# Differential attention in a four-layer sandwich: PSUM banks moved from the scores for the exponentials to the natural scores

## The reference

```
q1, k1, q2, k2, v = split(x @ Wqkv)      # 16 heads of 8; v: 16 heads of 16
A1 = softmax(mask(q1 k1^T / sqrt(8))) v  # causal, 1024 x 1024 per head and batch
A2 = softmax(mask(q2 k2^T / sqrt(8))) v
diff = A1 - lam * A2
out  = rmsnorm(diff per head) * (1 - lambda_init) @ Wproj
```

## Time and profile before

| | us |
|---|---|
| median of 3 runs | 1840.18 |
| lowest and highest | 1839.37, 1842.9 |
| the profiled execution, its own time | 1842.77 |
| its span, first to last instruction | 1841.0 |

### The profile page before, as it was taken

The page is one execution under the profiler, slowest core; times in us unless marked ns, Lnnn a source line. Parts: engine busy times, 40 slices in busy tenths (PEclk is TensorE's granted clock), DMA queues, the critical chain, the costliest instruction groups (busy, mean ns, idle before and its releaser), DMA issues. The chain is left out here.

```text
span 1841.0 us, 29946 instructions
## 1 busy us (share of the span) xinstructions
PE 1528.2 (83%) x8470; PEld 1026.0 (56%) x8532; DVE 1297.8 (70%) x3447; ACT 1086.2 (59%) x2348; POOL 1095.9 (60%) x1272
## 2 busy tenths in 40 slices
PE   4758989989989974377885789999999999989798
PEld 2413333333333323256563578888888888877566
DVE  5458777777777712483426599999999999984443
ACT  1104666666666661030222389999999999996241
POOL 5211456556456474301324399999999999984253
PEclk9858999999999996698998899999999999999899
DMA  3310100100101000383210000000000010000000
GB/s 114 120 51 24 32 19 24 29 18 25 28 18 25 12 1 1 126 274 103 92 46 1 1 1 1 1 1 1 1 1 1 1 46 1 1 1 1 1 23 23
DMA packets 39162, 59.48 MB, mean 32 GB/s; under 512 B 8700, under 2 KB 33160, under 8 KB 38152
## 3 DMA queue, kind: packets, MB, share of 16 engines
q1 hardware_dynamic: 39048, 58.12, 9.9%
HBM read 40.93 MB, written 16.78 MB: 31 GB/s over the span
## 5 line engine op out<-in xcount | busy, mean ns | idle before, releaser
L1896 POOL TENSOR_SCALAR c_R<-c_Z,c_negtau 128x256 f32<-128x256 f32 x519 | 589.0, 1167 | 53.3 <-DVE c_negtau L1965 30.8
L588 ACT ACTIVATE a_PT<-a_sc 128x512 f32<-128x512 f32 x576 | 316.3, 602 | 258.2 <-PE a_sc L653 174.9
L493 DVE TENSOR_REDUCE a_mpart<-a_nat 128x1 f32<-128x512 f32 (+3 forms) x640 | 378.0, 632 | 124.8 <-PE a_nat L620 78.4
L1851 ACT ACTIVATE c_R<-c_Z,c_negtau 128x256 f32<-128x256 f32 x1017 | 425.5, 515 | 5.2 <-DVE c_negtau L1965 3.4
L1932 DVE BATCH_NORM_STATS2 c_stat<-c_R 128x6 f32<-128x512 f32 x576 | 380.8, 678 | 2.7 <-ACT c_R L1851 2.7
L617 PE MATMUL a_nat<-KS,QS 96*128 96x512 bf16 (+3 forms) x768 | 253.5, 348 | 78.2 <-DVE a_mpart L493 44.9
L460 POOL TENSOR_SCALAR_AFFINE_SELECT a_PT<-a_PT 128x512 f32<-128x512 f32 x128 | 79.1, 636 | 265.1 <-ACT a_PT L588 265.1
L1768 PE MATMUL c_z<-mem,c_R 128*128 128x256 f32 x1024 | 231.5, 379 | 0.0
L1768 PEld LDWEIGHTS c_z<-mem,c_R 128*128 128x128 f32 x1024 | 193.1, 190 | 25.4
L653 PE MATMUL a_sc<-QS,KS 128*128 128x512 bf16 (+3 forms) x706 | 194.3, 324 | 3.9 <-ACT a_PT L588 2.9
L617 PEld LDWEIGHTS a_nat<-KS,QS 96*128 96x128 bf16 x768 | 74.5, 98 | 201.1 <-DVE a_mpart L493 161.0
(11 more groups left out here) (319 smaller groups left out, 2238.1 us busy)
## 6 DMA issues: line engine op xcount, KB each, us to landing
qk_parts<-a_parts SPq DMA_DIRECT2D x4, 1536.0 KB, 5.9
QS<-qk_parts SPq DMA_DIRECT2D x192, 32.0 KB
KS<-qk_parts SPq DMA_DIRECT2D x192, 32.0 KB
made<-m_made SPq DMA_DIRECT2D x24, 256.0 KB, 4.0
mem<-made SPq DMA_DIRECT2D x3, 2048.0 KB, 8.2
X<-in_L_attn_x_dram SPq DMA_DIRECT2D x1, 2048.0 KB, 8.5
ternary<-a_W_T SPq DMA_DIRECT2D x1, 2048.0 KB, 6.3
mem<-in_L_ffn_wq_dram SPq DMA_DIRECT2D x1, 2048.0 KB, 14.6
```

Source lines behind the costliest of these rows:

```text
L493: dve.tensor_reduce(mpart[:, b, j:j + cnt, i, k0 // 512], src, AX.X, ALU.max).then_inc(s_max, 1)
L588: act.activation(PT[:, n % 3, c, :], sc[:, u % 3, :], ACT.Exp, scale=SCALE0).then_inc(s_exp, 1)
L1851: act.activation(split(i, h) if r < NR else whole(i, h), Z[:, slot(i), h, :], ACT.Relu, bias=threshold(i, r, h)).then_inc(s_ra[r], 1)
L1896: pool.tensor_scalar(split(i, h) if r < NR else whole(i, h), Z[:, slot(i), h, :], threshold(i, r, h), 0.0, ALU.add, ALU.max).then_inc(s_rp ...
```

## The change

The tile `nat` gets three PSUM banks instead of two, and `sc` two instead of three; the sum stays eight banks. A unit now waits for the reduction three before, a score for the exponential two before. Since 40 is no multiple of 3, the bank of a unit is counted over the heads (`h.k` is the head's place in the loop).

```diff
-        nat, sc, OT, misc = ps("nat", [P, 2, 512]), ps("sc", [P, 3, 512]), ps("OT", [P, T]), ps("misc", [P, 512])
+        nat, sc, OT, misc = ps("nat", [P, 3, 512]), ps("sc", [P, 2, 512]), ps("OT", [P, T]), ps("misc", [P, 512])
...
-                src = nat[:, u % 2, 0:cnt * w].rearrange("p (a w) -> p a w", a=cnt)
+                src = nat[:, (NU * h.k + u) % 3, 0:cnt * w].rearrange("p (a w) -> p a w", a=cnt)
...
-                        act.activation(PT[:, n % 3, c, :], sc[:, u % 3, :], ACT.Exp, scale=SCALE0).then_inc(s_exp, 1)
+                        act.activation(PT[:, n % 3, c, :], sc[:, u % 2, :], ACT.Exp, scale=SCALE0).then_inc(s_exp, 1)
...
-                if not isinstance(h.n, int) or NU * h.n + u > 1:
-                    pe.wait_ge(s_max, h.count(NU, u - 1))
+                if not isinstance(h.n, int) or NU * h.n + u > 2:
+                    pe.wait_ge(s_max, h.count(NU, u - 2))
...
-                    out = nat[:, u % 2, s * w:(s + 1) * w]
+                    out = nat[:, (NU * h.k + u) % 3, s * w:(s + 1) * w]
...
-                if not isinstance(h.n, int) or 4 * NCH * h.n + u > 2:
-                    pe.wait_ge(s_exp, h.count(4 * NCH, u - 2))
+                if not isinstance(h.n, int) or 4 * NCH * h.n + u > 1:
+                    pe.wait_ge(s_exp, h.count(4 * NCH, u - 1))
...
-                    ins = pe.matmul(sc[:, u % 3, col:col + w], KS[:, h.buf, j, b * T + kt * P:b * T + (kt + 1) * P],
+                    ins = pe.matmul(sc[:, u % 2, col:col + w], KS[:, h.buf, j, b * T + kt * P:b * T + (kt + 1) * P],
```

## The result

| | before | after |
|---|---|---|
| median (lowest to highest), four runs each, us | 1841.54 (1839.37 to 1842.96) | 1791.21 (1788.79 to 1792.48) |
| profiled execution, own time / span | 1842.77 / 1841.0 | 1788.79 / 1787.0 |
| TensorE busy, VectorE busy | 1528.2, 1297.8 | 1519.5, 1288.3 |
| mean granted TensorE clock | 0.936 | 0.943 |

The ratio is 0.9716, 95% interval 0.9701 to 0.9731: **faster by 50.3 us**. The forecast was 38.3 faster, 1802, with a range from 1792. The sign and the mechanism held, the size did not: one stretch was priced at a seventh of its worth. The result lies just under the range, where rival 1 had put it (1791), and the first question is whether for its reason.

A forecast was written before the change was run, and what follows sets the result against it. No engine is full; TensorE idles 5.5 of 34.3 us a period, waiting mainly for VectorE to free natural banks. Savings 36.4 + 2.0 + 1.0 - 1.1 = 38.3 us gave a 1802 median, range 1792 to 1817.

The forecast's parts named there:

- rival 1: New waits for ScalarE and GpSimd hardly show, so 3.6 us a period is saved: 1791 us, chance 0.10.
- So the third bank of `sc` is not used up, and the second of `nat` is too few: Attention stage: TensorE's natural scores wait for VectorE 312 times; nearly all 61 score waits for ScalarE cost nothing.
- The replay of the period: One attention period of nine matmul groups, replayed with the new bank waits: 3.0 us saved of 34.26, chance 0.64.
- Group 9: Five units after VectorE's split, 4.31 us before: two come at once, four later waits stay, 0.25 saved.
- I take a new wait of 0.2 a period: Values of chunk 7 wait for GpSimd's mask: 0.2 us a period, between 0 and 0.6.
- The units before 165 us are mostly bound by VectorE or a load: 1.0, between 0 and 1.5.: Natural units ahead of the periods: the third bank saves only 1.0 us there, between 0 and 1.5.
- In head 0's period ... 2.0: First head's period, without VectorE's outputs between: group 7 saves only 0.24 us, the period 2.0.
- In the last head ... a loss of 1.1: Last head, no units to save on: groups grow by 0.54 us, mostly covered by GpSimd waits; 1.1 lost.
- Late work elsewhere: Rival: GpSimd's chain, or VectorE behind it, costs 1.0 us a period more: 1815 us, chance 0.18.
- the score ring deciding: Rival: TensorE's waits for exponentials in each group outweigh the gain, 4.9 us a period against 3.6: about 1857, chance 0.04.
- no change: Rival: TensorE's waits only turn into others, VectorE being the true bound: 1840 us, chance 0.03.
- The clock one: Rival: a tenth of the stretch at the lower, half-speed clock level costs 40 us: 1842, chance 0.01.

The follow-up runs named there:

- e3: The changed kernel with natural units waiting as with two banks throughout, so both rings use two: 1841.77 us, ratio 1.0001 to the kernel before.
- e1: The changed kernel with natural units waiting as with two banks in the ramp (ahead of the first exponential) only: 1798.11 us, ratio 0.9761 to the kernel before.
- e2: The changed kernel with the third natural bank used in the ramp only, two in the periods: 1833.61 us, ratio 0.9959 to the kernel before.
- e5: The changed kernel with GpSimd's ternary block in two parts, earlier, behind the masks of chunks 0 and 2: 1782.68 us, ratio 0.9700 to the kernel before.
- e4: The changed kernel with VectorE's outputs (reciprocal and product) moved behind the ninth unit of the next head: 1790.94 us, ratio 0.9721 to the kernel before.
- e6: The changed kernel with both the moves of e4 and e5, outputs later and ternary block earlier: 1781.95 us, ratio 0.9696 to the kernel before.
- e7: The kernel before, with only VectorE's reciprocal and product moved as in e4: 1829.01 us, ratio 0.9953 to the kernel before.

## Why the prediction was right, and where it was wrong

- *"So the third bank of `sc` is not used up, and the second of `nat` is too few"*: right. e3 puts the one at about nothing, and e1 and e2 share the 50 us of the other between the ramp and the periods.
- *The replay of the period*: right in eight of nine groups to 0.07 us, and in the starts of c0 and c1. Its sum was 31.5 with the wait for GpSimd, and the measured period is 31.44. That this fits so closely is partly luck: group 9 was 0.28 too short in it and the wait 0.2 too long, and the two cancel.
- *Group 9*: 4.06 forecast, 4.34 measured. VectorE's split took 1.37 us before (376.50 to 377.87). It took 1.57 after, and VectorE went into it without the pause of 0.91 that it had in the kernel before, so no cushion took the difference up. e5, where the split is 0.25 shorter and nothing else in the group differs, has 4.09; e4 and e6, where the outputs are elsewhere and the pause is back, have 4.06 and 3.96.
- *"I take a new wait of 0.2 a period" for GpSimd*: the place was right, the values of chunk 7 start 16.3 after group 7, where 16.25 was worked out, but the wait is hardly there: 0.05 in one period of three (group 2: 3.50 for 3.45). e4 shows that the slack is used up: ask for the values sooner and the wait grows by nearly as much as had been won.
- **The step that failed**: *"The units before 165 us are mostly bound by VectorE or a load: 1.0, between 0 and 1.5."* It is worth 7.1 by the trace, about 8 by e1 and 7.6 by e2. The bound was read from merged rows, which looked like work without a gap, and the bank's round trip that the replay used in the periods was never worked out at the lower clock level, where a matmul of 512 columns takes 0.43 instead of 0.22. There the two-bank ring allowed 0.70 a unit against VectorE's 0.56. Over the 40 units of head 0 this is 27.59 - 22.40 = 5.2, and 1.9 more on those of the next head.
- *"In head 0's period ... 2.0"*: 3.2 up to the first copy of the sums. 2.1 of it lie behind the first block of values, as forecast; 1.2 lie ahead of it (the next score starts at 157.98 and 148.36, 8.51 and 7.35 after the first exponential). Part of the 1.2 is the clock's: the upper level came about 3.5 us after the first exponential before and 2.3 after it now (0.74 granted from 152.50 to 153.50 before, 0.84 from 143.00 to 144.00 after, 0.50 just ahead of either). In e1 and e4, which have the change in this stretch and where it came 3.5 and 3.7 us after, it took 35.72 and 35.83 to the first copy for 35.18, so this part is some 0.6 at most, an estimate. The rest wasn't taken apart.
- *"In the last head ... a loss of 1.1"*: nothing lost and nothing gained, 57.30 and 57.34 from the 14th copy of the sums to the 16th. The groups did grow, from 2.40 to 2.89 each, but the waits for GpSimd's masks took it up: they fell from 1.84 and 4.46 to 0.69 and 2.54. The cover that the text claimed for the first four groups covered about all. e5 confirms that it is GpSimd's chain: with the ternary block out of it the head is 2.3 to 2.8 shorter.
- *The rivals*. Rival 1 gave 1791, the time measured, for a reason that is mostly false: the wait for GpSimd indeed hardly shows, but those for ScalarE do, and the period is not 3.6 shorter but 2.9. The number fits by luck: the periods saved 9 us less than it says, the ramp and the ends 9 more. Late work elsewhere (1815), the score ring deciding (1857) and no change fell with the first rows. The clock one fell with the granted clock, which stays at its upper level from 143.3 to 638.2. The Trainium skill, page "TensorE: Matmul & The Clock Gate", section "A second HAM failure mode: psum-queue depth-cycling", tells of a kernel whose TensorE, cycling through PSUM banks, stopped often and briefly and swung between its clock levels. With rings of two and of three banks this one does not, over the 495 us after and 532 us before.
- *The range* ended at 1792 because it carried bounds for the periods, worked out to 0.3 us, and for the ramp a bound of 1.5 taken without a row. It was said to take in rival 1 for the most part, although that rival's own 1791 lay outside. Where the long part is known well, the short part that was only looked at sets the error.

## What to carry to other kernels

Count a ring of buffers by its round trip, from the start of the work that fills a bank to the moment it is free, and do it again for every stretch with another clock or another shape; here the trip of two banks was 1.17 us at the upper level (0.42 + 0.75, 0.59 a unit, about VectorE's pace) and 1.40 at the lower one (0.70 a unit, well over it). A merged row is not an engine at work: divide its time by its count and compare with the duration of one operation back to back. And when a wait is removed, ask which engine sets the moment at the other end; here an added bank also bought what a reordering of VectorE's work would have bought alone (e7, 0.9 a period), so that the two do not add.

## What had not been expected of the hardware

The same small operation on VectorE can take more than twice as long. The rows of the split and of the product, after (GpSimd busy all the while) and in e6 (GpSimd without work from 375.43 to 383.56):

```profile
380.70 0.40 DVE L514 TENSOR_TENSOR a_mrest<-a_mrest,a_msplit 32x128 f32<-32x128 f32 x1
```

```profile
378.42 0.28 DVE L522 TENSOR_TENSOR a_mrest<-a_mrest,a_msplit 32x128 f32<-32x128 f32 x1
...
383.16 0.24 DVE L532 TENSOR_SCALAR a_rec<-a_rec,neglam 128x16 f32<-128x16 f32 x1
```

The subtraction of 32x128 took 0.40 and 0.28, the product of 128x16 0.66 (376.27, above) and 0.24. In the kernel before the subtraction took 0.28 with GpSimd busy beside it, so it is not a matter of GpSimd's being at work alone. For the product the ten profiles, with 160 of them, have a pattern. 98 times it began within 0.2 us behind the start of a mask or of an operation on two tensors of GpSimd's, and every time it ended 0.03 behind the end of that operation (begun at the same moment as a mask, it took 0.66, begun 0.10 later, 0.56). 46 times GpSimd was idle, and it took 0.23 or 0.24. It looks as if it waited for the operation to end, though in the 16 that are left it mostly took 0.23 beside an operation that had run longer. The Trainium skill, page "GPSIMD Engine Reference", section "1. Specifications", says that GpSimd shares its SBUF interfaces with VectorE, and that instructions of VectorE that have two SBUF inputs or run in a 2-port mode contend for them. The subtraction (L514) has two such inputs and would agree; the product has one large input and a scalar by partition, and whether it runs in a 2-port mode no row shows. What decides it was not tried.

In the ramp of before the granted clock stays at 0.50, although TensorE is busy for 34.87 of 40.00 us (108.70 to 148.70). After, its matmuls follow each other nearly without a pause at first (busy 12.51 of 12.60 us), then the clock rises for a moment and falls back (the columns: stretch, its length, busy us and count of PE, PEld, DVE, ACT and POOL, granted clock, DMA share, GB/s):

```profile
107.40:120.00 12.60, 12.51 (x44) 4.12 (x44) 11.61 (x21) 0.00 (x0) 0.00 (x0) 0.52 0.21 59
120.00:124.00 4.00, 2.84 (x11) 0.76 (x11) 4.00 (x8) 0.00 (x0) 0.00 (x0) 0.85 0.00 0
124.00:128.00 4.00, 4.00 (x12) 0.90 (x12) 4.00 (x8) 0.00 (x0) 0.00 (x0) 0.50 0.00 0
```

VectorE has no idle time in the second and third of these, so this rise gave the time nothing. e4 and e5, with the same ramp, had no such rise (0.50 throughout) and took 33.59 and 33.58 for it: the gain of the ramp is the ring's, and the rise isn't bound to the change.
